# Linear attention in a decoder layer: denominators on 32 partitions each, spread over 64 partitions by eight transfers on chip

## The chip, the cores and the metric

The kernel is one program on one core of a Trainium2 chip. The core has a matrix engine (TensorE, PE in the profile), a vector engine (VectorE, DVE), a scalar engine (ScalarE, ACT), a general engine (GpSimd, POOL), and a queue (SyncE, SP) that issues the transfers. Each works through its own list in order, and semaphores tie the lists together. The metric is the device time of one launch in microseconds (us); lower is better.

## What is computed

A decoder layer: linear attention with a decay, cross-attention, a mixture of experts, each with a residual and a layer norm. Only the linear attention is touched. For x of shape (16, 256, 256), 16 heads of 64:

```python
q, k = elu(x @ Wq) + 1, elu(x @ Wk) + 1          # per head, 64 wide
v = x @ Wv
a = sigmoid(x @ Wa + ba + 2.0)                   # one decay per token and head
def step(carry, inp):                            # over the 256 tokens
    S, z = carry
    S = a * S + outer(k, v)
    z = a * z + k
    num = einsum('bhk,bhkv->bhv', q, S)
    den = einsum('bhk,bhk->bh', q, z) + 1e-6
    return (S, z), num / den
out = concat_heads(num / den) @ Wo
x1 = layernorm(x + out)
```

The kernel unrolls the recurrence into a masked matrix per sequence and head: `probs[key, query] = (k . q) * exp(c_query..key)`, causal. The numerator of a query is `values^T @ probs`. The denominator is the sum of `probs` over the keys, one number per query and head. It has to stand on all 64 partitions of the head when the numerator (64 partitions by 256 queries) is divided by it.

## The kernel before

`linear_attention` (from L142) works on one sequence at a time, `b` from 0 to 15, and within it on one pair of heads at a time, `g` from 0 to 7: 128 steps, each of them one pass of the loop `for g in range(PAIRS)` on every engine. A pair fills the 128 partitions: head 0 on partitions 0 to 63, head 1 on 64 to 127. The order on each engine is the order of the code; nothing is rescheduled.

What each engine does in step (b, g), in this order:

- **TensorE** (L739): the scores of pair g (L706); parts of the next sequence's values (L656) in steps 1 and 2; for the pair before, `weighted_values`: numerators (L719), then denominators of queries 0 to 127 (L722) and, after a wait for `keys_summed`, of queries 128 to 255 (L725); the output projection of the pair three before (L735, `add_y`); the projection of q and k for the next sequence (L656, `project_qk`).
- **ScalarE** (L466): four exponentials that make the decays of pair g (L438, L440); `high_oT`, the rounded copy of the quotient of the pair two before (L457); `invert_den` for the pair before: `Ln` (L447) and `Exp` with scale -1 (L451), which write `rden`; then `exp_qk`, two passes over the next sequence's q and k (L413, L414).
- **VectorE** (L598): `normalise` of the pair two before (L569: numerator times `rden`, into `oT`), `finish_qk` (L554), `weigh` of pair g (L561, twice: scores times decays). Residual, statistics and scaling come in steps 2 and 4.
- **GpSimd** (L378): masks of the two decays (L362), the sum of two key blocks (L371), the low part of the quotient (L376).
- **SyncE** (L312): in each step one load of 256 KB that copies two rows of the summed decays to all 128 partitions (`spread_c`, L309), four buffers deep; five other transfers per sequence.

The denominators are made by a matmul whose stationary side is a block of ones, `ones`, 128 by 64, so that each of the 64 output partitions of a head gets the same sum. `ps_o[g % 2]` holds a pair's numerators in `[:, 0, :]` and its denominators in `[:, 1, :]`, 128 partitions by 256 queries each. `ps_o`, `rden` and `oT` have two buffers, used in turn.

`normalise` waits for `rden_done`, `high_oT` for `oT_done`, `weigh` and the scores for one another through `s_made`, `probs_done` and `o_made`.

## Time and profile before

| | us |
|---|---|
| median of 3 runs | 1423.08 |
| lowest, highest | 1421.81, 1424.44 |
| time of the profiled execution | 1418.74 |
| its span in the trace | 1416.9 |

The profiled execution is 4.3 us below the median of the three timed runs. Inside the span the linear attention takes the first 710 us; the 128 steps run from 45.7 us (the first `weigh`) to some 706 us. The profile gives for each instruction its start, its duration and, where its engine stood idle before it, what ended that idle time. Matmuls are pipelined and their ends are modelled, so the distance between two starts says more of them than a duration. The trace shows for a transfer how long SyncE was held by the issue, and for many of them the time from issue to landing. "PEclk" is the clock that TensorE was granted as a share of 2.4 GHz.

### The profile page before, as it was taken

Reading aid. Unit: us, or ns where it says so; the run is one execution under the profiler, and the core shown is the slowest. Engines: PE = TensorE matmul, PEld = TensorE weight load, DVE = VectorE, ACT = ScalarE, POOL = GpSimd, SP = SyncE. Lnnn points to the kernel's source line nnn. Section 1 sums busy time; section 2 is a strip of 40 time slices with the busy share of each in tenths; the row PEclk is TensorE's granted clock in tenths of the full one; section 3 lists DMA queues with packets and bytes.
Section 4 is the critical chain, followed back from the end, with each engine's and each line's share of the span. In section 5 each row is a group of like instructions: output and inputs, shape, how many; then the busy total and the mean of one; then the engine's idle time right before and its main releaser. Section 6 shows DMA issues by size and latency. Waiting matters only on the chain. (4 is left out here: it accounts for less than half of the span.)

```text
span 1416.9 us, 30100 instructions
## 1 busy us (share of the span) xinstructions
PE 1279.9 (90%) x10053; PEld 1077.0 (76%) x10053; DVE 832.9 (59%) x1643; ACT 952.1 (67%) x2120; POOL 734.5 (52%) x835
## 2 busy tenths in 40 slices
PE   5899999999999999999889999953599999998780
PEld 4788888888888888888767777743488888888780
DVE  4344555544555545555468888847366666666564
ACT  4677777777777777777747777754465666655453
POOL 0244444444444444444648777720467777776653
PEclk9999999999999999999999999975699999999895
DMA  4333222122222222222133433323356666666737
GB/s 153 94 102 85 86 80 79 62 81 78 84 76 76 61 84 75 84 70 75 61 117 83 117 104 97 95 76 96 115 130 157 157 164 157 158 161 152 183 62 244
DMA packets 155791, 151.30 MB, mean 107 GB/s; under 512 B 48882, under 2 KB 124250, under 8 KB 155674
## 3 DMA queue, kind: packets, MB, share of 16 engines
q1 hardware_dynamic: 140698, 129.18, 30.1%
q0 software_dynamic: 14976, 20.62, 8.1%
q8 instruction: 66, 1.08, 0.3%
q14 instruction: 51, 0.42, 0.1%
HBM read 113.45 MB, written 33.84 MB: 104 GB/s over the span
## 5 line engine op out<-in xcount | busy, mean ns | idle before, releaser
L362 POOL TENSOR_SCALAR_AFFINE_SELECT a_decay<-a_decay 128x256 f32<-128x256 f32 x256 | 110.2, 434 | 250.2 <-ACT a_decay L440 250.2
L561 DVE TENSOR_TENSOR a_probs<-a_ps_s,a_decay 128x384 f32<-128x384 f32 x256 | 135.0, 554 | 160.4 <-PE a_ps_o L725 121.5
L371 POOL TENSOR_TENSOR a_key_sum<-a_probs 128x256 f32<-128x256 f32 x128 | 97.3, 760 | 158.0 <-DVE a_probs L561 158.0
L1843 POOL DMA_INDIRECT sum_rows<-e_y_out,e_target x78 | 126.1, 1617 | 80.4 <-ACT e_y_out L1897 56.6
L413 ACT ACTIVATE a_qk_exp<-a_ps_qk 128x512 f32<-128x512 f32 x128 | 76.6, 599 | 130.8 <-PE a_ps_qk L656 124.0
L554 DVE SCALAR_TENSOR_TENSOR a_qk<-a_qk_exp,a_qk_relu 128x512 f32<-128x512 f32 x128 | 90.1, 704 | 114.7 <-ACT a_qk_relu L414 114.5
L656 PE MATMUL a_ps_qk<-a_xT_hi,a_w_hi 128*128 128x256 f32 x512 | 144.7, 283 | 4.9 <-ACT a_qk_relu L414 3.9
L656 PE MATMUL a_ps_qk<-a_xT_lo,a_w_hi 128*128 128x256 f32 x512 | 143.6, 280 | 0.0
L656 PE MATMUL a_ps_qk<-a_xT_hi,a_w_lo 128*128 128x256 f32 x512 | 143.6, 280 | 0.0
L438 ACT ACTIVATE a_decay<-a_c_rows,a_c_col 128x256 f32<-128x256 f32 x256 | 129.6, 506 | 0.0
L1824 POOL DMA_INDIRECT e_x_in<-x_rows,e_index x78 | 80.3, 1030 | 80.2 <-DVE e_index L1989 57.7
L706 PE MATMUL a_ps_s<-a_qk 64*128 64x256 f32 (+1 forms) x1024 | 118.2, 349 | 3.2 <-DVE a_probs L561 3.2
L706 PEld LDWEIGHTS a_ps_s<-a_qk 64*128 64x128 f32 x1024 | 88.6, 186 | 32.8 <-issue 21.0
L719 PE MATMUL a_ps_o<-a_probs,a_values 128*64 128x256 f32 (+1 forms) x1024 | 111.5, 339 | 0.4 <-DVE a_probs L561 0.4
L656 PEld LDWEIGHTS a_ps_qk<-a_xT_hi,a_w_hi 128*128 128x128 f32 x512 | 97.7, 191 | 6.8 <-issue 5.4
L440 ACT ACTIVATE a_decay<-a_c_rows,a_c_col 128x128 f32<-128x128 f32 x256 | 101.1, 395 | 0.0
L656 PEld LDWEIGHTS a_ps_qk<-a_xT_lo,a_w_hi 128*128 128x128 f32 x512 | 97.3, 190 | 0.0
L656 PEld LDWEIGHTS a_ps_qk<-a_xT_hi,a_w_lo 128*128 128x128 f32 x512 | 97.3, 190 | 0.0
L376 POOL TENSOR_TENSOR a_oT_lo<-a_oT,a_oT_hi 128x256 fp32r<-128x256 f32 x128 | 94.1, 736 | 1.2 <-ACT a_oT_hi L457 1.2
L719 PEld LDWEIGHTS a_ps_o<-a_probs,a_values 128*64 128x64 f32 x1024 | 62.2, 136 | 41.5 <-issue 11.4
L1002 POOL TENSOR_TENSOR b_probs<-b_probs,b_top 128x1232 f32<-128x1232 f32 x32 | 72.7, 2272 | 36.9 <-DVE b_top L1197 36.9
L2085 PE MATMUL e_ps_y<-e_dn_hi,e_hid_hi 128*128 128x256 f32 x312 | 88.5, 284 | 3.0 <-DVE e_hid_lo L2005 2.2
(297 smaller groups left out, 3871.6 us busy)
## 6 DMA issues: line engine op xcount, KB each, us to landing
a_c_rows<-a_c_scratch SPq DMA_DIRECT2D x128, 256.0 KB, 3.1
e_gu_raw<-in_L_ffn_gate_w SPq DMA_DIRECT2D x23, 512.0 KB
e_gu_raw<-in_L_ffn_up_w SPq DMA_DIRECT2D x23, 512.0 KB
e_dn_raw<-in_L_ffn_down_w SPq DMA_DIRECT2D x23, 512.0 KB, 5.5
a_x_in<-in_x SPq DMA_DIRECT2D x16, 256.0 KB, 2.7
a_x_res<-in_x SPq DMA_DIRECT2D x16, 256.0 KB
x_rows<-a_x SPq DMA_DIRECT2D x16, 256.0 KB, 3.3
x_bo_rows<-a_x_bo SPq DMA_DIRECT2D x16, 256.0 KB, 3.9
```

The source lines that it names most:

```text
L362: pool.affine_select(out=d, in_=d, compare_op=ALU.is_ge, fill=0.0, base=0, pattern=[[0, 2], [1, P]], channel_multiplier=-1)\
L371: pool.tensor_tensor(key_sum[:], probs[:, :, P:N], probs[:, :, N:TRI], ALU.add).then_inc(keys_summed, 1)
L376: pool.tensor_tensor(oT_lo[g % 2][:], oT[g % 2][:], oT_hi[g % 2][:].bitcast(F32), ALU.subtract).then_inc(oT_lo_done, 1)
L438: act.activation(decay[h][:, 0:N], rows[:, h, :], ACT.Exp, bias=c_now[:, 0, head:head + 1], scale=-1.0)
L440: act.activation(decay[h][:, N:TRI], rows[:, h, P:N], ACT.Exp, bias=c_now[:, 1, head:head + 1], scale=-1.0).then_inc(decay_exp[h], 1)
L554: vec.scalar_tensor_tensor(qk[g][:], qk_exp[:], 1.0, qk_relu[:], ALU.min, ALU.add).then_inc(qk_done, 1)
L561: vec.tensor_tensor(probs[:, h, :], ps_s[h][:, 0:TRI], decay[h][:], ALU.mult)\
L656: mm = pe.matmul(out, l, r, start=(n == 0), stop=(n == len(todo) - 1))
L706: mm = pe.matmul(ps_s[h][:, out], qk[g][rows, 1, j], qk[g][rows, 0, i], start=True, stop=True)
L719: pe.matmul(out[h][:, 0, cols], values[par][:, j, 2 * g + h, :], probs[:, h, keys], start=(j == 0), stop=(j == 1), skip_group_check=True)
L1843: pool.indirect_dma_start(sum_dram, bass.IndirectOffsetOnAxis(target[par][:, blk:blk + 1], 0), y_out[par][:, blk, :], None, compute_op=ALU ...
L2085: mm = pe.matmul(ps_y[n][:, 0:D], h[:, f, rows], w[par][:, f, :], start=(s == 0), stop=(s == len(todo) - 1))
```

## The change

**Denominators.** `ones` is 128 by 32 instead of 128 by 64. A pair's four sums (head 0 with queries 0 to 127, head 0 with queries 128 to 255, and the same for head 1) go to four groups of 32 partitions, all in the same 128 columns of `ps_o[g % 2][:, 1, 0:P]`. The number of matmuls stays four. All four now stand behind the wait for `keys_summed`; before, the first two stood ahead of it.

**Inverses.** `invert_den` works on 128 by 128 instead of 128 by 256, into `rden_row`.

**Spreading.** `spread_den` on SyncE waits for `rden_done` and issues eight transfers from `rden_row` to `rden`, 32 partitions by 128 numbers each (16 KB): two for each of the four blocks, one for each half of a head's 64 partitions. `normalise` waits for all eight (`rden_spread`, 128 per pair), no longer for `rden_done`.

**Order.** On VectorE `normalise` stands behind `finish_qk`. On SyncE each step begins with `spread_den`; `spread_c` loads one pair further ahead of its use in program order (four loads ahead of the loop instead of three), behind `spread_den`.

```diff
+    DENS = P // 4
-        ones, scan_ones = sb("a_ones", [P, DH]), sb("a_scan_ones", [H, N])
+        ones, scan_ones = sb("a_ones", [P, DENS]), sb("a_scan_ones", [H, N])
-        ln_den, rden = sb("a_ln_den", [P, N]), [sb(f"a_rden{n}", [P, N]) for n in range(2)]
+        ln_den, rden_row = sb("a_ln_den", [P, P]), [sb(f"a_rden_row{n}", [P, P]) for n in range(2)]
+        rden = [sb(f"a_rden{n}", [P, N]) for n in range(2)]
...
+            def spread_den(n):
+
+                sp.wait_ge(rden_done, n + 1)
+                if n >= 2:
+                    sp.wait_ge(oT_done, n - 1)
+                for t in range(4):
+                    h, half = t // 2, t % 2
+                    for first in range(h * DH, (h + 1) * DH, DENS):
+                        sp.dma_start(rden[n % 2][first:first + DENS, half * P:(half + 1) * P],
+                                     rden_row[n % 2][t * DENS:(t + 1) * DENS, :]).then_inc(rden_spread[n % 2], 16)
...
                 for g in range(PAIRS):
-                    ahead = b * PAIRS + g + ROWS_AHEAD - 1
-                    if g and ahead < B * PAIRS:
-                        spread_c(ahead // PAIRS, ahead % PAIRS)
-                    if g == 0:
-                        if b + 2 < B:
-                            load_x(b + 2)
-                        if ahead < B * PAIRS:
-                            spread_c(ahead // PAIRS, ahead % PAIRS)
+                    n = b * PAIRS + g
+                    spread_den(n)
+                    if g == 5 and b + 1 < B:
+                        spread_c(n + ROWS_AHEAD - 1)
+                    if g != 4 and n + ROWS_AHEAD < B * PAIRS:
+                        spread_c(n + ROWS_AHEAD)
+                    if g == 0 and b + 2 < B:
+                        load_x(b + 2)
...
-                act.activation(ln_den[:], ps_o[g % 2][:, 1, :], ACT.Ln, bias=den_eps[:]).then_inc(ln_done, 1)
+                act.activation(ln_den[:], ps_o[g % 2][:, 1, 0:P], ACT.Ln, bias=den_eps[:]).then_inc(ln_done, 1)
...
-                act.activation(rden[g % 2][:], ln_den[:], ACT.Exp, scale=-1.0).then_inc(rden_done, 1)
+                act.activation(rden_row[g % 2][:], ln_den[:], ACT.Exp, scale=-1.0).then_inc(rden_done, 1)
...
-                vec.wait_ge(rden_done, n + 1)
+                vec.wait_ge(rden_spread[g % 2], 128 * (n // 2 + 1))
...
+                    if g == 0 or has(b, 1):
+                        finish_qk(*projected_before(b, g))
                     if exists(b, g, 2):
                         before, _, pair = back(b, par, g, 2)
                         normalise(before, pair)
-                    if g == 0 or has(b, 1):
-                        finish_qk(*projected_before(b, g))
                     weigh(b, g)
...
-                for h in range(2):
-                    pe.matmul(out[h][:, 1, 0:P], ones[:], probs[:, h, 0:P], start=True, stop=True)
+                dens = [ps_o[g % 2][t * DENS:(t + 1) * DENS, 1, 0:P] for t in range(4)]
                 pe.wait_ge(keys_summed, n + 1)
                 for h in range(2):
-                    mm = pe.matmul(out[h][:, 1, P:N], ones[:], key_sum[:, h, :], start=True, stop=True)
+                    pe.matmul(dens[2 * h], ones[:], probs[:, h, 0:P], start=True, stop=True, tile_position=(0, 2 * h * DENS))
+                    mm = pe.matmul(dens[2 * h + 1], ones[:], key_sum[:, h, :], start=True, stop=True, tile_position=(0, (2 * h + 1) * DENS))
                 mm.then_inc(o_made, 1)
```

Three places where the lists of the engines differ. The names in brackets are the semaphores that an instruction waits for; "x7" is seven alike in a row.

SyncE, in the first sequence around the store of the next sequence's summed decays. Before:

```order
L309 DMA a_c_rows<-a_c_scratch 128x512 [waits a_decay_exp1] x3
L299 DMA a_c_scratch<-a_cT 16x256 [waits a_c_summed]
L309 DMA a_c_rows<-a_c_scratch 128x512 [waits a_decay_exp1,a_c_stored]
L309 DMA a_c_rows<-a_c_scratch 128x512 [waits a_decay_exp1] x2
L285 DMA a_x_in<-in_x 128x2x256 [waits a_xT_made]
```

Now:

```order
L312 DMA a_rden<-a_rden_row 32x128 [waits a_oT_done,a_rden_done]
L312 DMA a_rden<-a_rden_row 32x128 x7
L302 DMA a_c_scratch<-a_cT 16x256 [waits a_c_summed]
L312 DMA a_rden<-a_rden_row 32x128 [waits a_oT_done,a_rden_done]
L312 DMA a_rden<-a_rden_row 32x128 x7
L323 DMA a_c_rows<-a_c_scratch 128x512 [waits a_decay_exp1,a_c_stored]
L323 DMA a_c_rows<-a_c_scratch 128x512 [waits a_decay_exp1]
```

Where one load per step stood alone, eight small transfers now stand ahead of it in every step.

VectorE, step 2 of the second sequence. Before:

```order
L569 TENSOR_TENSOR a_oT<-a_ps_o,a_rden 128x256 [waits a_oT_lo_done,a_rden_done]
L554 SCALAR_TENSOR_TENSOR a_qk<-a_qk_exp,a_qk_relu 128x512 [waits a_s_made,a_qk_kept]
L561 TENSOR_TENSOR a_probs<-a_ps_s,a_decay 128x384 [waits a_decay_masked0,a_o_made,a_s_made]
L561 TENSOR_TENSOR a_probs<-a_ps_s,a_decay 128x384 [waits a_decay_masked1]
L575 TENSOR_TENSOR a_resid<-a_ps_y,a_x_res 128x512 [waits a_x1_ready,a_x_res_loaded,a_y_added]
```

Now:

```order
L568 SCALAR_TENSOR_TENSOR a_qk<-a_qk_exp,a_qk_relu 128x512 [waits a_s_made,a_qk_kept]
L583 TENSOR_TENSOR a_oT<-a_ps_o,a_rden 128x256 [waits a_oT_lo_done,a_rden_spread0]
L575 TENSOR_TENSOR a_probs<-a_ps_s,a_decay 128x384 [waits a_decay_masked0,a_o_made,a_s_made]
L575 TENSOR_TENSOR a_probs<-a_ps_s,a_decay 128x384 [waits a_decay_masked1]
L589 TENSOR_TENSOR a_resid<-a_ps_y,a_x_res 128x512 [waits a_x1_ready,a_x_res_loaded,a_y_added]
```

The quotient has moved from the head of the step to just before the two products of `weigh`, and waits for the transfers.

TensorE, `weighted_values` and the start of `add_y` in a step of the second sequence. Before:

```order
L719 MATMUL a_ps_o<-a_probs,a_values 64x256 [waits a_probs_done0,a_probs_done1,a_oT_done,a_v_done]
L719 MATMUL a_ps_o<-a_probs,a_values 64x256
L719 MATMUL a_ps_o<-a_probs,a_values 64x128 x2
L722 MATMUL a_ps_o<-a_probs,a_ones 64x128 x2
L725 MATMUL a_ps_o<-a_key_sum,a_ones 64x128 [waits a_keys_summed]
L725 MATMUL a_ps_o<-a_key_sum,a_ones 64x128
L735 MATMUL a_ps_y<-a_wo_hi,a_oT_hi 128x256 [waits a_oT_lo_done,a_resid_done]
```

Now:

```order
L733 MATMUL a_ps_o<-a_probs,a_values 64x256 [waits a_probs_done0,a_probs_done1,a_oT_done,a_v_done]
L733 MATMUL a_ps_o<-a_probs,a_values 64x256
L733 MATMUL a_ps_o<-a_probs,a_values 64x128 x2
L738 MATMUL a_ps_o<-a_probs,a_ones 32x128 [waits a_keys_summed]
L739 MATMUL a_ps_o<-a_key_sum,a_ones 32x128
L738 MATMUL a_ps_o<-a_probs,a_ones 32x128
L739 MATMUL a_ps_o<-a_key_sum,a_ones 32x128
L749 MATMUL a_ps_y<-a_wo_hi,a_oT_hi 128x256 [waits a_oT_lo_done,a_resid_done]
```

The same four denominators, 32 output partitions wide instead of 64, with the wait ahead of the first.

## Rows read from the trace of the kernel before

**Rows 1.** Windows: stretch, then busy us (instructions) of PE, PEld, DVE, ACT, POOL; PEclk, DMA share, GB/s.

```profile
46.00:666.00 620.00, 620.00 (x5436) 516.69 (x5435) 320.02 (x639) 474.84 (x1184) 270.13 (x466) 1.00 0.26 79
666.00:706.00 40.00, 36.26 (x356) 29.64 (x355) 20.53 (x45) 30.32 (x81) 24.22 (x43) 1.00 0.25 80
707.00:714.00 7.00, 4.78 (x43) 4.42 (x41) 3.70 (x12) 4.76 (x12) 1.15 (x4) 1.00 0.08 27
938.00:945.00 7.00, 3.45 (x21) 2.64 (x19) 1.69 (x5) 4.15 (x12) 0.00 (x0) 0.80 0.22 75
```

**Rows 2.** Timeline of DVE: start, us, line, tiles, [idle before, releaser]; `weigh` and last quotient.

```profile
45.70 1.02 DVE L561 TENSOR_TENSOR a_probs<-a_ps_s,a_decay 128x384 f32<-128x384 f32 x2 [0.40 <-POOL a_decay L362]
...
678.17 1.14 DVE L561 TENSOR_TENSOR a_probs<-a_ps_s,a_decay 128x384 f32<-128x384 f32 x2 [0.67 <-POOL a_decay L362]
...
702.50 1.02 DVE L561 TENSOR_TENSOR a_probs<-a_ps_s,a_decay 128x384 f32<-128x384 f32 x2 [2.08 <-PE a_ps_o L725]
703.44 0.41 DVE L569 TENSOR_TENSOR a_oT<-a_ps_o,a_rden 128x256 f32<-128x256 f32 x1
705.97 0.42 DVE L569 TENSOR_TENSOR a_oT<-a_ps_o,a_rden 128x256 f32<-128x256 f32 x1 [2.12 <-ACT a_rden L451]
709.34 0.69 DVE L575 TENSOR_TENSOR a_resid<-a_ps_y,a_x_res 128x512 f32<-128x512 f32 x1 [2.94 <-PE a_ps_y L735]
```

**Rows 3.** Timeline of ACT, one step and two places of the last sequence.

```profile
499.30 0.40 ACT L440 ACTIVATE a_decay<-a_c_rows,a_c_col 128x128 f32<-128x128 f32 x1
499.59 0.40 ACT L457 CAST a_oT_hi<-a_oT 128x256 fp32r<-128x256 f32 x1
499.89 0.48 ACT L447 ACTIVATE a_ln_den<-a_ps_o,a_den_eps 128x256 f32<-128x256 f32 x1
500.40 0.42 ACT L451 ACTIVATE a_rden<-a_ln_den 128x256 f32<-128x256 f32 x1
...
695.60 0.41 ACT L457 CAST a_oT_hi<-a_oT 128x256 fp32r<-128x256 f32 x1 [1.33 <-DVE a_oT L569]
695.91 0.47 ACT L447 ACTIVATE a_ln_den<-a_ps_o,a_den_eps 128x256 f32<-128x256 f32 x1
...
703.89 0.41 ACT L457 CAST a_oT_hi<-a_oT 128x256 fp32r<-128x256 f32 x1 [0.52 <-DVE a_oT L569]
```

**Rows 4.** Groups of ACT instructions by line: busy us, mean ns, idle before.

```profile
L438 ACT ACTIVATE a_decay<-a_c_rows,a_c_col 128x256 f32<-128x256 f32 x250 | 126.5, 506 | 0.0
L440 ACT ACTIVATE a_decay<-a_c_rows,a_c_col 128x128 f32<-128x128 f32 x250 | 98.7, 395 | 0.0
```

**Rows 5.** Timeline of SyncE: transfers in a row, and one alone.

```profile
721.25 0.59 SPq L954 DMA_DIRECT2D x_rows<-b_spare  x1
721.88 0.45 SPq L955 DMA_DIRECT2D sum_rows<-b_spare  x1
722.37 0.45 SPq L954 DMA_DIRECT2D x_rows<-b_spare  x1
722.86 0.45 SPq L955 DMA_DIRECT2D sum_rows<-b_spare  x1
...
754.56 5.40 SPq L938 DMA_DIRECT2D b_v_now<-b_v_scratch  x12
...
499.72 0.34 SPq L309 DMA_DIRECT2D a_c_rows<-a_c_scratch  x1
```

**Rows 6.** Transfers of single lines: ns on SyncE min/median/max, first and last start.

```profile
L309 SPq DMA_DIRECT2D a_c_rows<-a_c_scratch x128: 319/320/856, 32.5 to 687.4; - x128
L938 SPq DMA_DIRECT2D b_v_now<-b_v_scratch x192: 231/328/1226, 742.0 to 921.1; - x192
```

**Rows 7.** DMA issues: count, KB each, median us from issue to landing.

```profile
a_c_rows<-a_c_scratch SPq DMA_DIRECT2D x128, 256.0 KB, 3.1
x_rows<-b_spare SPq DMA_DIRECT2D x4, 130.0 KB, 2.1
sum_rows<-b_spare SPq DMA_DIRECT2D x4, 128.0 KB, 1.9
a_c_scratch<-a_cT SPq DMA_DIRECT2D x16, 16.0 KB, 1.5
```

**Rows 8.** Timeline of TensorE weight loads around the denominators of one step.

```profile
503.17 0.25 PEld L722 LDWEIGHTS a_ps_o<-a_probs,a_ones 128*64 128x64 f32 x4
503.39 0.25 PEld L725 LDWEIGHTS a_ps_o<-a_key_sum,a_ones 128*64 128x64 f32 x4
503.82 0.19 PEld L735 LDWEIGHTS a_ps_y<-a_wo_hi,a_oT_hi 128*128 128x128 f32 x1 [0.17 <-issue]
```

**Rows 9.** Timeline of TensorE matmuls as the clock rises from 0.50 to 1.00.

```profile
1011.65 0.63 PE L2073 MATMUL e_ps_g<-e_xT_hi,e_gu_lo 128*128 128x512 f32 x1
1012.07 0.63 PE L2073 MATMUL e_ps_g<-e_xT_hi,e_gu_hi 128*128 128x512 f32 x1
...
1015.24 0.39 PE L2073 MATMUL e_ps_g<-e_xT_lo,e_gu_hi 128*128 128x512 f32 x1
1015.47 0.39 PE L2073 MATMUL e_ps_g<-e_xT_hi,e_gu_lo 128*128 128x512 f32 x1
```

More of the change, by code:

```diff
@@ L337, in _ @@
             store_c(0)
-            for g in range(ROWS_AHEAD - 1):
-                spread_c(0, g)
+            for n in range(ROWS_AHEAD):
+                spread_c(n)
             for b in range(B):
```

5 lines of the change are left out of this document (3 added, 2 removed).

## The prediction

> **What bounds the kernel now.** First the windows. From 46 to 666 us TensorE is busy for all 620 us, ScalarE for 475 (77%), VectorE for 320, GpSimd for 270, and TensorE has its full clock of 2.4 GHz [rows 1]. So in the stretch where each step also projects the next sequence, TensorE's own work sets the step. Then the timeline of VectorE, to get the step. The first `weigh` of sequence 0 starts at 45.70, that of sequence 15 at 678.17 [rows 2]: 120 steps in 632.5 us, **5.27 us a step**. In the last sequence, without projections, `weigh` goes on to 702.50 [rows 2]: seven steps of 3.48 us. There TensorE is busy for 36 of 40 us [rows 1]. From the last `weigh` to the residual sum of sequence 15 (709.34) pass 6.84 us [rows 2]. Everything behind that is another stage, which the change doesn't touch.
>
> The question of this change is not how busy an engine is. It is whether a chain from one step to the next becomes longer than 5.27 us. Such a chain is in the code. ScalarE's order in a step is `high_oT` of pair n-1, then `invert_den` of pair n. `high_oT` of pair n-1 waits for the quotient of pair n-1, which waits for the inverse of pair n-1. So the inverse of pair n can't start before that of pair n-1 has been used. Before, that costs nothing: an inverse ends, the quotient follows on VectorE 0.04 us later (2.12 us of waiting for it only in the drained end [rows 2]), and the whole round takes under 2 us.
>
> **The change part by part.**
>
> *The round trip.* The chain now goes ScalarE `Exp`, SyncE, eight transfers, VectorE quotient, ScalarE `high_oT`, `Ln`, `Exp`. Its terms, in us:
> - `Exp` ends, SyncE starts: 0.02 (L440 ends at 499.70 [rows 3], the load that waits for it is issued at 499.72 [rows 5]).
> - Eight issues in a row. SyncE is held 0.32 by a transfer issued alone [rows 6], and the next starts 0.04 after an end; in a row each holds it 0.45 and starts come every 0.49 [rows 5]. A dozen small ones in a row took 5.40, 0.45 each [rows 5]. The cost of an issue hardly depends on the bytes, so I take it for 16 KB too. From the first start to the eighth: 0.36 + 6 x 0.49 = 3.30.
> - The eighth from issue to landing: no row shows a small transfer within the chip's own memory. The nearest are 1.5 for 16 KB issued alone, and 1.9 to 2.1 for 128 KB issued in a row [rows 7]. The size is that of the first, the place in a row that of the second: I take 1.7.
> - Landing to the start of the quotient: 0.05; the quotient: 0.42 [rows 2].
> - Quotient ends to `high_oT`: 0.04 (703.44 + 0.41 to 703.89 [rows 2, 3]). `high_oT` to `Ln`: 0.31 (695.60 to 695.91 [rows 3]).
> - `Ln` start to `Exp` start is 0.51, `Exp` 0.42 [rows 3]. On 128 columns instead of 256 each is shorter by 0.11, the difference of 506 and 395 ns between the two decay exponentials [rows 4]: 0.40 and 0.31.
>
> Transfers 5.00, the rest 1.55: **6.55 us a round**, one round a step.
>
> *Does anything hide it?* `normalise` of pair n-1 stands on VectorE ahead of `weigh` of pair n+1, so while it waits, `weigh`, and behind that the scores and TensorE's whole next step, are held up: it cannot run more than a step ahead. Between an `Exp` and the next `high_oT` ScalarE has only `exp_qk` and the decays to do, and both fit in 5 us. The move of `normalise` behind `finish_qk` buys what `finish_qk` waits for; it takes nothing from the round, since `high_oT` stands ahead of the next inverse all the same. So all of it lies on the path, and TensorE, with 5.27 us of work, waits 1.28 us a step.
>
> *SyncE itself.* Per step eight issues and one or two loads, 4.2 to 4.7 us, within 6.55: it does not bind by itself. The loads stand behind the eight, so their 3.1 us [rows 7] run while nobody waits; their buffers are four deep, and the added waits in the queue are older than the one it already waits for.
>
> *ScalarE.* Two operations lose 0.11 us each: 0.22 x 128 = 28 us of busy time. It was not the bound; the 0.22 stands in the round already.
>
> *TensorE.* The matmuls stay four, of the same columns. The weight loads of the two pairs of denominators start 0.22 apart, and 0.65 after the first comes `add_y` [rows 8]. If the four groups of 32 run side by side where two groups of 64 did, 0.22 us a step are saved; if not, nothing. The `keys_summed` wait is older than the first denominator either way. With TensorE waiting 1.28 us a step, both are worth zero here. The row before `add_y` shows an idle 0.17 us where the stationary side goes from 64 to 128 columns [rows 8], 115 times in the main stretch. The Trainium skill, page "TensorEngine Tiling (Array Packing)", Key Properties, says that changing the tiling mode drains TensorE; the trace agrees with that 0.17 us, and going from 64 to 32 columns would be one more such change, which leaves 0.05 of the 0.22 us. It matters only where TensorE still sets the step.
>
> *Sum.* Main stretch 120 x (6.55 - 5.27) = 153.6. Last sequence 7 x (6.55 - 3.48) = 21.5. The end: the last `weigh` starts 0.5 after the transfers of the pair two before have landed; two rounds and 3.4 us (705.97 to 709.34 [rows 2]) later comes the residual sum. That is 2 x 6.55 + 2.9 = 16.0 instead of 6.84, or 9.2 more. In all **+184 us** on 1418.7, so 1603 for the profiled execution. The median of the timed runs lay 4.3 above it: **1607**.
>
> *Bounds.* Issues 0.45 apart and a landing of 1.4 (below the smallest median) give a round of 6.0 and +115 us, 1538. Issues 0.49 apart and 2.2 give 7.05 and +249 us, 1672. With 3.1, the landing of the 256 KB loads, it would be 7.95 and some +370 us, 1790: the far end, and these transfers have a sixteenth of the bytes.
>
> **The rivals.**
>
> *Issues at their fastest.* The shortest issue in the trace held SyncE for 0.231 us [rows 6]. If eight small ones come every 0.27, they and a landing of 1.5 take 3.4, the round 4.95, under TensorE's 5.27. The main stretch stays, the last sequence costs 7 x 1.5 = 10 and the end 6: 1439. For it: the transfers are two-dimensional and on chip. Against it: the median of that same line is 0.328, and its dozen in a row came every 0.45.
>
> *The transfers are hidden, and the kernel gets faster.* This decides below a round of 5.27, with the four column groups side by side: 120 x 0.22 = 26 us less, 5 given back at the end, 1402. It needs issues some 0.2 apart, closer than any row. With the extra drain it gives 1420, no change. The Trainium skill, page "DMA: Bandwidth & Descriptors", section "Issuing engines are not separate DMA queues", says that initiating a DMA is usually small relative to the DMA itself; by that the round would be near 3.6 and this rival would hold. The rows speak against it, since eight issues at 0.49 outweigh a landing of 1.5 to 2.1.
>
> *TensorE's clock falls.* With 1.3 us of waiting a step TensorE is busy for some 80% in the main stretch and half in the last sequence. A stretch with 4.78 busy of 7 us had 1.00, one with 3.45 of 7 us had 0.80 [rows 1]. At 1.2 GHz the same matmuls start 0.42 instead of 0.23 apart [rows 9], the step would be near 9.8 us, and TensorE the bound again: +570 us, about 2000. Against it: the main stretch would be busier than the one that had 1.00. In the last sequence a fall costs little, since its 3.1 us of work doubled still fit in a round.
>
> **How the numbers follow.** A round of 6.0 to 7.1, set by the transfers: 0.80. Issues at their fastest, slower by 1 to 2%: 0.07. Hidden, faster 0.04, no change 0.03. Clock 0.03. A round above 7.1: 0.03. The range reaches from 1500, with some room below the lower bound (steps that carry the values' projections are longer and may absorb part of the round), to 1690. A measurement of this kernel can tell about 0.2% (3 us) from no change. Faster 0.04, same 0.03, slower 0.93.
>
> **What would show it.** Right: `weigh` starts some 6.5 us apart in the main stretch and the last sequence alike; ScalarE's idle time before `high_oT` is ended by the quotient, that of VectorE before the quotient by the transfers; TensorE is busy for about 80%; the eight issues span 3.3 us, and 1.7 us later the quotient starts. If the spacing stays 5.3, the issues are cheap. If TensorE's granted clock is 0.5 in the main stretch, the third rival holds. The prediction is wrong if the issues are not spaced by 0.45 to 0.49, if the landing is outside 1.4 to 2.2, or if ScalarE's chain is not what `high_oT` waits in.

## The result, and the profile after

The changed kernel took **1789.59 us** (median of 4 runs, 1788.11 to 1790.72) against 1422.44 us before (median of 4). It is slower by a quarter: the ratio is 1.258, with a 95% interval of 1.2557 to 1.26. The prediction said 1607, at most 1690. Its direction and its mechanism were right, and the size was not: the kernel lost 367 us where 184 were forecast. The span of the profiled execution grew from 1416.9 to 1786.3 us, by 369.4.

First the length of a step. Timeline of VectorE after, the first, the 121st and the last `weigh`, and the end, to be held against [rows 2]:

```profile
45.65 1.02 DVE L575 TENSOR_TENSOR a_probs<-a_ps_s,a_decay 128x384 f32<-128x384 f32 x2 [0.40 <-POOL a_decay L376]
...
1003.22 1.01 DVE L575 TENSOR_TENSOR a_probs<-a_ps_s,a_decay 128x384 f32<-128x384 f32 x2
...
1058.68 1.01 DVE L575 TENSOR_TENSOR a_probs<-a_ps_s,a_decay 128x384 f32<-128x384 f32 x2
1065.98 0.42 DVE L583 TENSOR_TENSOR a_oT<-a_ps_o,a_rden 128x256 f32<-128x256 f32 x1 [6.28 <-DMA a_rden<-a_rden_row]
1074.30 0.42 DVE L583 TENSOR_TENSOR a_oT<-a_ps_o,a_rden 128x256 f32<-128x256 f32 x1 [7.89 <-DMA a_rden<-a_rden_row]
1077.80 0.69 DVE L589 TENSOR_TENSOR a_resid<-a_ps_y,a_x_res 128x512 f32<-128x512 f32 x1 [3.08 <-PE a_ps_y L749]
```

120 steps take 957.6 us, 7.98 each (5.27 before), and the seven of the last sequence 7.92 each (3.48). From the last `weigh` to the residual sum pass 19.1 us (6.84). That is 120 x 2.71 = 325, 7 x 4.45 = 31 and 12, in all 368 of the 369 us: the whole loss lies in the 128 steps and their end. That both kinds of step have the same length, with and without TensorE's projections, already says that TensorE doesn't set it.

Now who waits for whom. Waits of the steps after the change (engine, line, releaser: us in total, times, longest us), 46 to 1080 us:

```profile
POOL a_key_sum L385 <- DVE a_probs L575: 622.7, 128, 6.8
DVE a_oT L583 <- DMA a_rden<-a_rden_row: 562.1, 128, 7.9
ACT a_oT_hi L471 <- DVE a_oT L583: 522.5, 127, 7.3
```

VectorE waits 128 times for the transfers, 4.4 us each time, and ScalarE 127 times for VectorE's quotient: the chain that the prediction described. One round of it, in the timelines of SyncE, VectorE and ScalarE:

```profile
566.26 4.94 SPq L312 DMA_DIRECT2D a_rden<-a_rden_row  x8
571.25 0.58 SPq L323 DMA_DIRECT2D a_c_rows<-a_c_scratch  x1
...
573.95 5.54 SPq L312 DMA_DIRECT2D a_rden<-a_rden_row  x8
...
564.76 0.42 DVE L583 TENSOR_TENSOR a_oT<-a_ps_o,a_rden 128x256 f32<-128x256 f32 x1 [4.57 <-DMA a_rden<-a_rden_row]
...
572.45 0.42 DVE L583 TENSOR_TENSOR a_oT<-a_ps_o,a_rden 128x256 f32<-128x256 f32 x1 [4.19 <-DMA a_rden<-a_rden_row]
...
580.68 0.42 DVE L583 TENSOR_TENSOR a_oT<-a_ps_o,a_rden 128x256 f32<-128x256 f32 x1 [4.51 <-DMA a_rden<-a_rden_row]
...
565.22 0.41 ACT L471 CAST a_oT_hi<-a_oT 128x256 fp32r<-128x256 f32 x1 [2.96 <-DVE a_oT L583]
565.53 0.36 ACT L461 ACTIVATE a_ln_den<-a_ps_o,a_den_eps 128x128 f32<-128x128 f32 x1
565.92 0.31 ACT L465 ACTIVATE a_rden_row<-a_ln_den 128x128 f32<-128x128 f32 x1
```

Read it as a sum. Quotient at 564.76, first issue at 566.26: 1.50. The eight issues last 4.94, each 0.59 but the first (0.51), with 0.04 between two; the eighth starts 4.35 after the first. From there to the next quotient at 572.45: 1.84. Round 7.69. The next round lasts 8.23, because its eight issues take 5.54: one of them held SyncE longer. The line of all 1024 issues (ns on SyncE min/median/max) and their landing, in the view of that source line:

```profile
L312 SPq DMA_DIRECT2D a_rden<-a_rden_row x1024: 507/591/1947, 51.5 to 1072.5; - x171
...
DMA to landing us min/median/max: 1.7/1.8/5.2
```

44 of them are above 0.7 us and 35 above 1.0; together they hold SyncE 33 us beyond the median, some 0.25 us a step. With a few late landings that fills the 0.29 between the undisturbed round and the mean step.

TensorE after, by windows [as rows 1]:

```profile
46.00:960.00 914.00, 691.42 (x5338) 534.39 (x5336) 332.75 (x624) 435.68 (x1159) 272.06 (x456) 0.89 0.23 69
960.00:1080.00 120.00, 71.78 (x497) 53.65 (x491) 32.24 (x65) 39.60 (x113) 31.77 (x57) 0.74 0.18 54
```

Busy for 76% of the main stretch instead of 100%, at a mean granted clock of 0.89 (by the two levels, 1.2 GHz for some 22% of it).

### The profile page after: what moved, and what is told of

The parts are those of the page before. It is cut to its first block and busy times, and to the rows that moved or that the text cites. A ratio compares the mean times of both kernels' runs of the same rounds, so it can differ in the third digit from the quotient of the medians.

```text
span 1786.3 us, 31250 instructions
## 1 busy us (share of the span) xinstructions
PE 1384.1 (77%) x10053; PEld 1116.2 (62%) x10053; DVE 854.9 (48%) x1643; ACT 919.8 (51%) x2120; POOL 742.7 (42%) x835
## 5 line engine op out<-in xcount | busy, mean ns | idle before, releaser
L720 PE MATMUL a_ps_s<-a_qk 64*128 64x256 f32 (+1 forms) x1024 | 143.2, 404 | 256.4 <-DVE a_probs L575 256.4
L583 DVE TENSOR_TENSOR a_oT<-a_ps_o,a_rden 128x256 f32<-128x256 f32 x128 | 54.3, 425 | 562.1 <-DMA a_rden<-a_rden_row 562.1
L471 ACT CAST a_oT_hi<-a_oT 128x256 fp32r<-128x256 f32 x128 | 51.9, 405 | 524.8 <-DVE a_oT L583 522.5
L720 PEld LDWEIGHTS a_ps_s<-a_qk 64*128 64x128 f32 x1024 | 112.9, 220 | 289.4 <-issue 284.8
L376 POOL TENSOR_SCALAR_AFFINE_SELECT a_decay<-a_decay 128x256 f32<-128x256 f32 x256 | 119.5, 471 | 133.5 <-ACT a_decay L454 131.1
L568 DVE SCALAR_TENSOR_TENSOR a_qk<-a_qk_exp,a_qk_relu 128x512 f32<-128x512 f32 x128 | 116.9, 913 | 85.3 <-ACT a_qk_relu L428 85.1
L733 PE MATMUL a_ps_o<-a_probs,a_values 128*64 128x256 f32 (+1 forms) x1024 | 143.2, 413 | 2.3 <-DVE a_probs L575 2.3
L575 DVE TENSOR_TENSOR a_probs<-a_ps_s,a_decay 128x384 f32<-128x384 f32 x256 | 129.5, 547 | 3.1 <-PE a_ps_o L739 2.6
L733 PEld LDWEIGHTS a_ps_o<-a_probs,a_values 128*64 128x64 f32 x1024 | 75.2, 165 | 60.5 <-issue 41.3
L749 PE MATMUL a_ps_y<-a_wo_hi,a_oT_hi 128*128 128x256 f32 x256 | 97.0, 379 | 9.0 <-POOL a_oT_lo L390 9.0
```

The lines of the kernel that those rows point to most:

```text
L376: pool.affine_select(out=d, in_=d, compare_op=ALU.is_ge, fill=0.0, base=0, pattern=[[0, 2], [1, P]], channel_multiplier=-1)\
L568: vec.scalar_tensor_tensor(qk[g][:], qk_exp[:], 1.0, qk_relu[:], ALU.min, ALU.add).then_inc(qk_done, 1)
L575: vec.tensor_tensor(probs[:, h, :], ps_s[h][:, 0:TRI], decay[h][:], ALU.mult)\
L720: mm = pe.matmul(ps_s[h][:, out], qk[g][rows, 1, j], qk[g][rows, 0, i], start=True, stop=True)
L733: pe.matmul(out[h][:, 0, cols], values[par][:, j, 2 * g + h, :], probs[:, h, keys], start=(j == 0), stop=(j == 1), skip_group_check=True)
L749: mm = pe.matmul(ps_y[:, blk, :], l[:, rows], r[:, g, :], start=(g == 0 and blk == 0 and n == 0), stop=(g == PAIRS - 1 and n == 2), skip_g ...
```

## The experiments

The theory: each pair's inverses now pass a closed round of three engines and eight issues, which is longer than TensorE's step. The rivals: SyncE is simply full; the four column groups or the new order cost something by themselves; the way over the chip is slow because of its landing, not of its issues; the traffic of 1024 more transfers slows the other work. All ratios are to the kernel before, measured on the same chip.

**The issues without anybody waiting for them.** The kernel before, with eight such transfers a step of numbers that nobody reads; the loads on SyncE stand as in the change.

```diff
+            def spare(n):
+                sp.wait_ge(rden_done, n + 1)
+                if n:
+                    sp.wait_ge(spare_sent, 128 * n)
...
+                        sp.dma_start(spare_out[first:first + P // 4, half * P:(half + 1) * P],
+                                     spare_in[t * (P // 4):(t + 1) * (P // 4), :]).then_inc(spare_sent, 16)
```

> The kernel before, with eight transfers of 32 partitions by 128 numbers added per step on SyncE, in the places of the change's, from and to tiles that nobody else reads or writes; nothing waits for them but the next step's eight. Theory A (the change is slow because the eight stand in a round that returns to ScalarE): no round here, so only SyncE's own occupancy can bind. In the changed kernel's trace an issue takes 0.63 us from start to start, so 8 x 0.63 + 0.63 for the load + some 0.3 for the rest = 6.0 us a step against 5.27: about +0.75 x 120 + 2.5 x 7 = +107 us, some 1530 us. Theory B (the 1024 transfers slow the other work by traffic, whoever waits): close to the changed kernel, 1750 to 1790.

1609.82 us, ratio 1.132 (1.1298 to 1.1343); steps of 6.64 us, 5.54 in the last sequence. SyncE, in the timeline:

```profile
521.56 4.95 SPq L310 DMA_DIRECT2D a_spare_out<-a_spare_in  x8
526.55 0.58 SPq L321 DMA_DIRECT2D a_c_rows<-a_c_scratch  x1
...
528.22 5.58 SPq L310 DMA_DIRECT2D a_spare_out<-a_spare_in  x8
```

SyncE hardly stops: eight issues, the load, and the others of the sequence take 6.66 us from one group to the next. The loads of the decays come late, and ScalarE's decays with them (160.7 us of waiting in 32 times). So SyncE alone, without the round, would have made the kernel slower by 13%. The prediction had it at 4.2 to 4.7 us a step, and this run's expectation at 6.0, 80 us too low. The run also waits for the eight before to have landed, which the change doesn't (43.7 us in 68 times); so it is an upper price of SyncE alone. And it doesn't fall on every step. By pair, the median distance of `weigh` to the next stays within 0.06 us of the one before in pairs 1 to 5 (7.33, 5.81, 4.72, 4.67, 4.06 us) and is 12.58 in pair 7 (5.19 before): SyncE falls behind during a sequence, the loads issued ahead hide it, and ScalarE waits some 9 us once a sequence. So the transfers' traffic, which is the same in every step, slows nothing that can be seen here.

**No transfers at all.** The changed kernel with `spread_den` left out. It leaves out the division: the quotient reads tiles set to one.

```diff
-                    spread_den(n)
...
+            pool.memset(rden[0][:], 1.0).then_inc(consts_step, 1)
+            pool.memset(rden[1][:], 1.0).then_inc(consts_step, 1)
...
-                vec.wait_ge(rden_spread[g % 2], 128 * (n // 2 + 1))
+                vec.wait_ge(rden_done, n + 1)
```

> The changed kernel with the eight transfers left out: the quotient reads tiles set to one at the start, so the attention isn't divided by its denominators; the quotient waits for ScalarE's inverse as before. It shows what the other parts (four column groups, half the work of the two ScalarE passes, the order on VectorE) are worth without the transfers. Theory A, with the changed trace's 1.15 us from the first numerator to the output projection instead of 1.24: 0.09 a step, 11 us in all, 1411 us. Rival: the four groups save the whole 0.22 a step, 1397 us. If the narrower groups cost a drain as large as what they save: 1423.

1408.72 us, ratio 0.990 (0.9873 to 0.9921). Steps of 5.15 and 3.42 us, and TensorE is busy for all of 619 us. This is all that the other parts of the change bring: 0.12 us a step of TensorE, and with the lists in this order it is the ceiling for any cheaper way of spreading. The whole loss, and 1% more, is the transfers'.

**The order alone.** The kernel before with `normalise` behind `finish_qk`.

```diff
+                    if g == 0 or has(b, 1):
+                        finish_qk(*projected_before(b, g))
                     if exists(b, g, 2):
                         before, _, pair = back(b, par, g, 2)
                         normalise(before, pair)
-                    if g == 0 or has(b, 1):
-                        finish_qk(*projected_before(b, g))
```

> The kernel before, with only the one move on VectorE: normalise behind finish_qk. The prediction's step: it takes nothing from TensorE's 5.27 us a step, so 1421, within 0.3% of before. Rival: the later quotient makes ScalarE's copy late and costs what the wait in the changed kernel seems to cost, 10 us or more.

1423.82 us, ratio 1.0007 (0.9997 to 1.0017), steps of 5.27 and 3.47: nothing, as predicted.

**What an issue costs.** The kernel before, with groups of eight transfers (four of the largest) of several shapes, in every second sequence another kind; they are issued after the inverse and nobody reads them. It ran once; only its trace is used.

```diff
+                    if b == 2:
+                        d = sp.dma_start(probe_out[q, i // 4, :], probe_in[q, :])
...
+                    if b == 6:
+                        d = sp.dma_start(probe_out[:, i, :], probe_in[:])
+                    if b == 8:
+                        d = sp.dma_start(probe_dram[i, 0:32, :], probe_in[q, :])
+                    if b == 10:
+                        d = sp.dma_start(probe_out[q, i // 4, :], probe_dram[i, 0:32, :])
```

> The kernel before, with transfers of one shape added per even sequence, each on its own line, which nobody waits for but the next step's: sequence 2 on chip 32 partitions x 512 B, 4 on chip 64 x 512 B, 6 on chip 128 x 512 B (four of them), 8 chip to DRAM 32 x 512 B, 10 DRAM to chip 32 x 512 B, 12 on chip 16 x 512 B, 14 falls to none of these but to chip to DRAM 128 x 512 B. Theory G (an issue costs more when both ends are on chip): 2, 4, 6 and 12 hold SyncE 0.59 us in a row, 8, 10 and 14 hold it 0.45. Rival H (the cost comes from the small shape): 2, 8 and 10 hold it 0.59 alike, 4, 6 and 14 less. Rival J (any eight in a row behind a semaphore, whatever they move): all 0.59.

By source line (ns on SyncE min/median/max): 16 KB on chip (L316), 64 KB on chip (L320), 16 KB from the chip to DRAM (L322), 16 KB from DRAM to the chip (L324).

```profile
L316 SPq DMA_DIRECT2D a_probe_out<-a_probe_in x64: 507/591/1842, 135.0 to 190.1; - x64
...
L320 SPq DMA_DIRECT2D a_probe_out<-a_probe_in x32: 465/601/1813, 327.5 to 366.8; - x32
...
L322 SPq DMA_DIRECT2D a_probe_dram<-a_probe_in x64: 302/421/1105, 412.2 to 455.1; - x64
...
L324 SPq DMA_DIRECT2D a_probe_out<-a_probe_dram x64: 302/421/1414, 498.5 to 542.0; - x64
```

And eight in a row, in the timeline of SyncE:

```profile
142.35 5.33 SPq L316 DMA_DIRECT2D a_probe_out<-a_probe_in  x8
...
412.24 3.59 SPq L322 DMA_DIRECT2D a_probe_dram<-a_probe_in  x8
...
512.18 3.55 SPq L324 DMA_DIRECT2D a_probe_out<-a_probe_dram  x8
```

With both ends on the chip an issue in a row holds SyncE 0.59 to 0.60 us, for 16 KB as for 64 KB; with one end in DRAM it is 0.42. The other three shapes fall in: 8 and 32 KB on chip 0.59 and 0.60, 64 KB from the chip to DRAM 0.43. The prediction's "hardly depends on the bytes" held; among these plain blocks it depends on where the two ends lie. It isn't the ends alone: further below, a store to DRAM of four rows that lie 32 partitions apart holds SyncE 0.53. Landings had medians of 1.8 (16 KB on chip), 2.0 (64 KB), 1.5 (to DRAM) and 1.7 us (from DRAM).

**The round opened.** The changed kernel with `high_oT` behind `invert_den` and `exp_qk`, so that an inverse no longer waits for the quotient of the pair before (`ln_den` has two buffers for it).

```diff
-                    if exists(b, g, 2):
-                        before, _, pair = back(b, par, g, 2)
-                        high_oT(before, pair)
                     if exists(b, g, 1):
                         before, _, pair = back(b, par, g, 1)
                         invert_den(before, pair)
                     if has(b, 1):
                         exp_qk(b + 1, g)
...
+                    if exists(b, g, 2):
+                        before, _, pair = back(b, par, g, 2)
+                        high_oT(before, pair)
```

> The changed kernel with one move on ScalarE: the rounded copy of the quotient (high_oT) stands behind the inverse and the two passes over q and k instead of ahead of the inverse; ln_den has two buffers for that. All eight transfers stay. Theory A: this breaks the round from step to step, so that the step is set by the next limit, SyncE's 6.0 us of issues (plus 0.3 for the issues that take twice as long now and then): 1417 + 120 x 0.9 + 7 x 2.7 + 6, about 1550 us. Theory B (traffic or the eight's latency as such): no change, 1790.

1591.13 us, ratio 1.119 (1.1173 to 1.121); steps of 6.45 and 6.49. One move in a list takes back 199 of the 367 us (1789.6 to 1591.1): the round was what set the step. The expectation, 1550, had SyncE at 6.0 to 6.3 us a step. What sets it now is in SyncE's own waits. After the change (60 to 1070 us), and then in this kernel (60 to 880 us):

```profile
SPq L312 <- ACT a_rden_row L465: 220.0, 125, 3.5
```

```profile
SPq L312 <- ACT a_rden_row L465: 23.6, 34, 1.7
```

```profile
515.34 5.79 SPq L312 DMA_DIRECT2D a_rden<-a_rden_row  x8
521.16 0.58 SPq L323 DMA_DIRECT2D a_c_rows<-a_c_scratch  x1
521.84 4.94 SPq L312 DMA_DIRECT2D a_rden<-a_rden_row  x8
```

SyncE has almost stopped waiting for the inverse; it goes from one group of eight to the next in 6.50 us, here with one slow issue. The second limit is SyncE's occupancy, and it lies where the first experiment found it.

**Four transfers instead of eight.** Half of the inverse tile stays one.

```diff
-                    for first in range(h * DH, (h + 1) * DH, DENS):
+                    for first in (h * DH + half * DENS,):
...
-                vec.wait_ge(rden_spread[g % 2], 128 * (n // 2 + 1))
+                vec.wait_ge(rden_spread[g % 2], 64 * (n // 2 + 1))
```

> The changed kernel with four of the eight transfers, one per denominator block (those whose source and target partitions are the same); the other half of each inverse tile stays at one, so half of the quotients aren't divided by their denominators. Theory A: a round of 1.50 + 0.55 + 2 x 0.633 + 1.84 = 5.16, with 0.15 for the slow issues 5.3 us, in the main stretch and the last sequence alike: 1421 + 20 + 13 + 7 = 1461 us. Rival (the landing, not the issues, is what made the step long): hardly less than 1790.

1492.52 us, ratio 1.050 (1.0468 to 1.0521). The last sequence has steps of 5.32 us, a round of 1.5 + 3 x 0.63 + 1.84 = 5.2 with its slow issues. The main stretch has 5.69, more than the sum expected. The reason is that steps differ. Median distance of `weigh` to the next, by pair, in us, worked out from the timelines:

| pair | 0 | 1 | 2 | 3 | 4 | 5 | 6 | 7 |
|---|---|---|---|---|---|---|---|---|
| before | 5.93 | 7.39 | 5.81 | 4.72 | 4.67 | 4.06 | 4.59 | 5.19 |
| no transfers | 5.79 | 7.24 | 5.65 | 4.64 | 4.34 | 4.20 | 4.47 | 5.08 |
| four transfers | 5.78 | 6.65 | 5.65 | 5.23 | 5.15 | 5.53 | 5.86 | 5.14 |
| after | 8.07 | 7.69 | 7.70 | 7.69 | 7.68 | 7.91 | 8.40 | 7.69 |

A round of 5.2 leaves the long steps of TensorE alone and stretches the short ones; a mean of 5.27 hides that. With each distance of the kernel without transfers raised to at least 5.2 the mean is 5.6, against 5.69 measured. The change's round of 7.69 is above every step, so there nothing was absorbed.

**One transfer.** The kernel before, its inverses of 128 by 256 sent in a single transfer of 128 KB on chip (no column groups); the order on SyncE and VectorE is the change's.

```diff
+            def spread_den(n):
+                sp.wait_ge(rden_done, n + 1)
+                if n >= 2:
+                    sp.wait_ge(oT_done, n - 1)
+                sp.dma_start(rden[n % 2][:], rden_row[n % 2][:]).then_inc(rden_spread[n % 2], 16)
...
-                vec.wait_ge(rden_done, n + 1)
+                vec.wait_ge(rden_spread[g % 2], 16 * (n // 2 + 1))
```

> The kernel before with denominators on 64 partitions each and 256 wide inverses, whose inverses go through one transfer on chip (128 partitions x 1 KB, same partitions) that the quotient waits for; the order on SyncE and VectorE is the changed kernel's. Theory A (the round is 1.5 us of engines plus the span of the issues plus one landing): 1.5 + 0.22 + 2.1 = 3.8 us, below TensorE's 5.27 a step, so only the last sequence (7 x 0.3) and the end (some 3 us) pay: 1426 us. Rival (a wait on a transfer in the round costs by itself, whatever their number): 1480 or more.

1433.92 us, ratio 1.008 (1.0064 to 1.01); steps of 5.28 in the main stretch. A round under TensorE's step costs the main stretch nothing. Its length stands in the last sequence, in VectorE's timeline:

```profile
704.32 0.42 DVE L577 TENSOR_TENSOR a_oT<-a_ps_o,a_rden 128x256 f32<-128x256 f32 x1 [2.32 <-DMA a_rden<-a_rden_row]
...
708.03 0.42 DVE L577 TENSOR_TENSOR a_oT<-a_ps_o,a_rden 128x256 f32<-128x256 f32 x1 [2.36 <-DMA a_rden<-a_rden_row]
...
711.76 0.42 DVE L577 TENSOR_TENSOR a_oT<-a_ps_o,a_rden 128x256 f32<-128x256 f32 x1 [2.37 <-DMA a_rden<-a_rden_row]
717.38 0.42 DVE L577 TENSOR_TENSOR a_oT<-a_ps_o,a_rden 128x256 f32<-128x256 f32 x1 [5.20 <-DMA a_rden<-a_rden_row]
```

3.7 us a round against 3.8 expected (`weigh` comes every 3.91 in the mean). The last quotient waits 5.2 us, and that is the landing. SyncE issued its transfer 0.03 us after the inverse had ended, and it took 3.9 us to land instead of 2.0; in SyncE's timeline, and among the issues from 713 to 718 us (KB, us to landing):

```profile
713.47 0.47 SPq L307 DMA_DIRECT2D a_rden<-a_rden_row  x1
```

```profile
a_rden<-a_rden_row SPq DMA_DIRECT2D x1, 128.0 KB, 3.9
```

The stores of the sequence's result, issued just ahead of it, had landed at 712.64 and 713.39. Why this landing was late is open.

**Two queues.** The changed kernel with four of the eight issued by ScalarE.

```diff
+        def issue_den(eng, n, parts):
...
+                issue_den(sp, n, (0, 1))
...
+                act.wait_ge(rden_done, n + 1)
+                issue_den(act, n, (2, 3))
```

> The changed kernel with the eight transfers issued by two engines: four by SyncE, four by ScalarE itself right behind its Exp. If the 0.63 us is the issuing engine's own time and the two don't hinder one another, ScalarE becomes the bound: its 3.8 us of work plus 4 x 0.63 are 6.3 us a step, so 1421 + 125 + 14 + 7, about 1570 us. If the issues of both go through one generator that takes 0.63 us each, the eight still span 4.4 us, the round is 7.7 or more, and the time 1790 or above.

1659.16 us, ratio 1.167 (1.1628 to 1.1713); steps of 7.06 and 5.71. Both queues issue side by side, in the timelines of SyncE and ScalarE:

```profile
506.57 2.41 SPq L281 DMA_DIRECT2D a_rden<-a_rden_row  x4
...
506.57 2.72 ACTq L281 DMA_DIRECT2D a_rden<-a_rden_row  x4
509.39 0.60 ACT L430 ACTIVATE a_qk_exp<-a_ps_qk 128x512 f32<-128x512 f32 x1 [2.85 <-issue]
```

So the 0.6 us belong to the queue that issues; they are not shared out among queues. But on ScalarE they are 2.85 us in which it computes nothing: 356.3 us ahead of `exp_qk` in the main stretch, 117 times. ScalarE had 4.0 us of work a step before (475 us in 118 steps [rows 1]); now it computes or issues for 6.58 of 7.06 us a step and is the bound. The expectation, 1570, had taken four issues at 2.5 us and a ScalarE without gaps. Half of the issues on a busy engine is a third limit.

**By way of DRAM.** One store of the four rows, a wait for it, and two loads that each spread one head's numbers over its 64 partitions: three issues.

```diff
-                for t in range(4):
...
+                sp.dma_start(den_dram[n % 2], rden_row[n % 2][0:P:DENS, :]).then_inc(den_stored, 16)
+                sp.wait_ge(den_stored, 16 * (n + 1))
+                for h in range(2):
+                    one_head = den_dram[n % 2, 2 * h:2 * h + 2, :].rearrange("(a t) i -> a (t i)", a=1)
+                    sp.dma_start(rden[n % 2][h * DH:(h + 1) * DH, :], one_head.to_broadcast([DH, N])).then_inc(rden_spread[n % 2], 16)
```

> The changed kernel with the inverses by way of DRAM (one store, a wait, two loads: three issues instead of eight), the order on ScalarE as it is in the change. All of the computation is done. Theory: the round closes as before, and is 1.5 for the engines + 1.5 landing of the store + 0.46 + 1.8 landing of the second load + 0.1 = 5.3 to 5.5 us; near TensorE's 5.15, where the two mix (the kernel with four transfers had a round of 5.3 and steps of 5.69): 5.4 to 5.7 main, 5.4 in the last sequence, 1455 to 1490 us, ratio 1.023 to 1.048. Rival (the number of issues alone counts, not the way through DRAM): three issues instead of four would be a round of 4.7 and 1425 or less.

1601.5 us, ratio 1.122 (1.1196 to 1.1252); steps of 6.51 and 6.28. Both expectations were too low. In the timelines of SyncE and VectorE:

```profile
575.63 0.52 SPq L311 DMA_DIRECT2D a_den_scratch<-a_rden_row  x1
577.22 1.10 SPq L315 DMA_DIRECT2D a_rden<-a_den_scratch  x2
...
574.12 0.43 DVE L585 TENSOR_TENSOR a_oT<-a_ps_o,a_rden 128x256 f32<-128x256 f32 x1 [2.94 <-DMA a_rden<-a_den_scratch]
...
580.61 0.42 DVE L585 TENSOR_TENSOR a_oT<-a_ps_o,a_rden 128x256 f32<-128x256 f32 x1 [2.98 <-DMA a_rden<-a_den_scratch]
```

574.12 to 575.63 is the 1.5 of the engines, 1.59 until the store has landed and the first load is issued, 0.51 to the second load, and then 2.88 here (2.66 in the median of all rounds) to the quotient. The expectation had taken 1.8, near the 1.7 of a plain 16 KB load, for it. A load of 64 KB in which 64 partitions read the same 1 KB lands after a median of 2.6 us. The round is 6.3 in the median and 6.5 in the mean.

**DRAM, with the round opened.** The same with `high_oT` late, as above.

> The changed kernel with two edits: the inverses travel through DRAM (one store of the four rows, a wait for its landing, then two loads that each spread one head's 256 numbers over 64 partitions: three issues instead of eight), and the copy of the quotient stands behind the inverse and the exponentials of q and k in ScalarE's list. All of the computation is done. Theory (the eight issues and the closed round are all that is wrong with the change): an issue with one end in DRAM holds SyncE 0.32 alone and 0.46 in a row in the issue-cost kernel, and lands after 1.5 (store) and 1.7 (load); so inverse to quotient takes 0.02 + 1.5 + 0.46 + 1.7 + 0.1 = 3.8 us, one step of 5.15 can cover it now that no round closes within a step, SyncE is held about 3 us a step with its wait, and TensorE sets the step as in the kernel without transfers: 5.15 to 5.2 in the main stretch, about 4.3 in the last sequence (two steps for a chain of 8.5), 1410 to 1420 us, ratio 0.993 to 1.0. Rival (the wait for the store's landing on SyncE keeps the other loads late, or the landings through DRAM grow to over 2 us each beside the other traffic): steps of 5.4 or more and 1445 or more.

1487.79 us, ratio 1.044 (1.0413 to 1.0457); steps of 5.62 and 5.39. The theory, which had hoped to beat both kernels, fell. From the end of an inverse to its quotient it takes 4.73 us at the least and 5.33 in the mean, against the 3.8 expected. And there is a second round, over two steps: quotient of pair n, `weigh` of pair n+2, its matmuls, its inverse, its transfers, its quotient. From a quotient to the end of that inverse the trace has 4.36 us at the least. At its shortest this round is 9.1 us for two steps, 4.55 a step, which is above TensorE's 3.42 in the last sequence and below its 5.15 in the main stretch. So it can set the last sequence; that it sets the steps of 5.62 isn't shown. Part of those is the order's doing, as the last kernel below shows.

**Four transfers, with the round opened.** Half of the inverse tile stays one.

> The kernel with four transfers and the copy of the quotient behind the inverse and the exponentials: half of the inverse tile stays one, so half of the output is not normalised. Theory: with the round no longer closed within one step and SyncE held 4 x 0.63 + 0.9 = 3.4 us a step, nothing but TensorE is left: 5.15 to 5.25 main, 4.3 last, 1412 to 1425, ratio 0.993 to 1.002. Rival (four transfers cost what the kernel with four showed whatever the order, because slow issues and late loads do it): 1480 or more.

1459.92 us, ratio 1.024 (1.0226 to 1.0259); steps of 5.46 and 4.35. The last sequence came out as expected, the main stretch not. In the waits from 60 to 700 us TensorE's weight loads and matmuls of `add_y` wait for the low part of the quotient, which `high_oT` now starts too late:

```profile
PEld a_ps_y L752 <- POOL a_oT_lo L393: 40.6, 71, 1.1
PE a_ps_y L752 <- POOL a_oT_lo L393: 22.5, 57, 0.8
```

**The late copy by itself.** That wait could be the transfers' doing or the order's. So: no transfers, and `high_oT` late.

> The kernel without transfers (inverse tile of ones, quotient waits for the inverse alone, output not normalised), and the copy of the quotient behind the inverse and the exponentials of q and k in ScalarE's list. It asks what the place of that copy costs by itself. Theory (the late copy makes TensorE wait): in the kernel with four transfers and the late copy TensorE and its weight loads waited for the low part of the quotient 118 times and 63 us between 60 and 700 us, against 0.8 us in the kernel without transfers and with the early copy; if that is the order's doing, the step is 5.15 + 0.2 to 0.5 = 5.35 to 5.6 here too, 1433 to 1460 us, ratio 1.007 to 1.025. Rival (it is the transfers' doing: the quotient comes late, so its low part does): no wait here, step 5.15, last sequence 3.4, 1409 us, ratio 0.99.

1440.53 us, ratio 1.013 (1.0102 to 1.0162); steps of 5.41 and 3.41. The same wait, with no transfer in the kernel:

```profile
PEld a_ps_y L751 <- POOL a_oT_lo L392: 44.9, 75, 0.7
PE a_ps_y L751 <- POOL a_oT_lo L392: 25.8, 61, 0.5
```

It is the order's: 32 us against the 1408.72 of the kernel with the early copy. `high_oT` stands between two needs. Ahead of the inverse it closes the round; behind `exp_qk` it makes TensorE wait. A place right behind the inverse, ahead of `exp_qk`, was not tried. Four transfers with the late copy lie 35 us over the kernel before, and the way through DRAM with the late copy 63; 19 of them stand in this kernel too, which has no transfer.

No kernel here beats the one before while it computes everything.

## Why the prediction was right and wrong

**The chain: right.** ScalarE waits for the quotient and VectorE for the transfers in every step; the two kinds of step have one length; opening the round gave back 199 us.

**The engines' share of the round: right.** 1.55 was worked out with 0.05 from landing to quotient. The rest of it, 1.50, was measured as 1.50, and 0.02 from the landing to the quotient.

**The landing: right.** 1.7 and 0.05 to the quotient taken, 1.84 measured, median landing 1.8.

**The spacing of the issues: wrong, and this is the step that failed.** The sum took 0.45 a piece and 0.49 from start to start, 3.30 to the eighth. Measured were 0.59, 0.63 and 4.35. That one term makes the undisturbed round 7.69 instead of 6.55 (with 0.09 of landing), and by the prediction's own sum 120 x 2.42 + 7 x 4.21 + 11.4 = 331 us instead of 184: 1754. The rows it was taken from [rows 5] were transfers with one end in DRAM, and the issue-cost kernel shows that this is what matters.

The trace of before had the number. The prediction said that no row showed a small transfer within the chip's own memory; for the landing it went to neighbours, and for the issues it never asked the question. But the next stage has a transfer from one tile on the chip to another, and its source line in the trace of before reads (ns on SyncE min/median/max, then landing):

```profile
L928 SPq DMA_DIRECT2D b_k_now<-b_k_all x15: 646/656/1124, 720.4 to 898.9; - x15
...
DMA to landing us min/median/max: 2.3/2.8/4.1
```

0.66 us each, alone, against 0.32 for a load from DRAM alone [rows 6]. (It cuts its tiles in another way than the change does, whose first issue of a group holds 0.51.) It even stands right ahead of the row quoted first in [rows 5], whose 0.59 was passed over for the three 0.45 behind it. With 0.66 + 0.04 seven times the sum would have been a round of 8.15 and 1814 us, 1.4% above the measured time.

**The slow issues: not foreseen.** One in 23 holds SyncE above 0.7 us, up to 1.95. In a round with eight issues on the path that adds 0.25 us a step; 0.29 a step over the undisturbed round is 37 us, the rest of the way from 1754 to 1790. The maxima 856 and 1226 ns in [rows 6] were the sign of it.

**SyncE's own occupancy: wrong, by the same term, without effect here.** 4.2 to 4.7 us a step were forecast; it is 5.6 with one load, and 6.45 in the kernel with the late copy. The change's round of 7.98 covers it, but it set the time of that kernel. A load behind an on-chip issue takes 0.58 instead of 0.32, which is part of it.

**The range: too narrow on the upper side.** Its bounds varied the landing from 1.4 to 3.1 and the spacing only from 0.45 to 0.49. The spacing enters seven times, the landing once; the term with the larger factor had the smaller bound, and it rested on the wrong kind of row. The round came out above 7.1, where the chance given was 0.03. That the far end (a round of 7.95, 1790 us) names the measured 7.98 and 1789.59 is luck: it had the round from a landing of 3.1 us, which didn't come.

**The order on VectorE, the loads: right.** Ratio 1.0007 for the order alone; in the trace after the change ScalarE never stands idle ahead of a decay once the steps have begun, so no load comes late.

**TensorE and the column groups: right, between the two values given.** 0.22 us a step was named if the groups run side by side and 0.05 with a further change of tiling mode. The kernel without transfers gains 0.12. In the timeline of the weight loads after, to be held against [rows 8]:

```profile
570.22 0.11 PEld L738 LDWEIGHTS a_ps_o<-a_probs,a_ones 128*32 128x32 f32 x1 [0.17 <-issue]
...
570.26 0.11 PEld L739 LDWEIGHTS a_ps_o<-a_key_sum,a_ones 128*32 128x32 f32 x1
570.57 0.19 PEld L749 LDWEIGHTS a_ps_y<-a_wo_hi,a_oT_hi 128*128 128x128 f32 x1 [0.20 <-issue]
```

The eight weight loads of four groups start within 0.05 us and `add_y` follows 0.35 after the first (0.65 before); but there is now an idle 0.17 us ahead of them too, which wasn't there before. 0.30 saved less 0.17 is 0.13, the 0.12 of the steps: the second change of mode was priced right, the saving a little low. That agrees with what the Trainium skill, page "TensorEngine Tiling (Array Packing)", Key Properties, says of a change of tiling mode.

**The clock: half right.** The main stretch was said to keep its full clock; the mean granted one fell to 0.89, and to 0.74 in the end of the steps. The stretch was busy for 76%, against 68% in the one of [rows 1] that had kept 1.00, so that comparison was no bound. It cost nothing that can be seen: in the stretch with 0.74 the quotients at 1058.34 and 1065.98 are 7.64 apart, an undisturbed round as at 566 us.

**Issues against landings.** That initiating a DMA is usually small relative to the DMA itself (the Trainium skill, page "DMA: Bandwidth & Descriptors", section "Issuing engines are not separate DMA queues") does not hold here: one issue holds SyncE 0.59 us, a third of the 1.8 to its landing, and eight in a row 4.94.

## What to carry to other kernels

Before N transfers are put between two engines, price N times the distance from one issue to the next plus one landing, and take that distance from a row with the same two ends (here 0.63 us on chip, 0.46 with DRAM at one end) and the same cut of its tiles, never from a row that is only alike in size. Then look for what else is in the lists: an instruction that waits for the result and stands ahead of the next start closes a round from step to step, and the queue's whole occupancy per step is a second limit right behind it. And compare a round with each step, not with the mean, since it stretches the short ones; a saving of 0.1 us a step on the bound engine does not pay for any of this.

## What the runs showed of the hardware

- An issue with both ends on the chip holds SyncE 0.59 us in a row (0.51 the first), for 16 and for 64 KB; with one end in DRAM 0.42 for plain blocks, but 0.53 for a store of four rows 32 partitions apart. Whatever is issued right behind an on-chip one is held 0.58 too, also a load from DRAM.
- The hold is per queue: SyncE and ScalarE issued four each at the same time, in 2.41 and 2.72 us.
- Of the change's 1024 issues 44 held SyncE over 0.7 us and 35 over 1.0, up to 1.95. Why is open.
- A load that spreads 1 KB of DRAM over 64 partitions lands after 2.6 us; plain loads of 16 KB after 1.7.
- Eight weight loads for four column groups of 32 start within 0.05 us, and entering that mode costs an idle 0.17 us.
